# Step lists for fill, steady and drain turns, finer steps, and no filler matmuls, in a ViT tower on one core

## The chip, the cores and the metric

The kernel runs on one core of one Trainium2 chip. The metric is device time in microseconds (us), lower is better; three runs of the kernel before gave 623.52, 623.66 and 624.88 us.

## What is computed

128 images of 3x64x64 pass two transformer layers at 17 tokens (16 patches and a class token) of width 192. Cut to what matters:

```python
h = patches @ W_tok.T + b                         # 16 patches of 768 values, then cls in front
h = h + attn0(layernorm(h))                       # 12 heads of 64
    # dots = q k^T * scale; se = mean over heads; diagonal masked; top 12 of 17 kept; + se; softmax; @ v; @ w_out
h = h + bitlinear_ffn(layernorm(h))               # rmsnorm, int8 activations, ternary weights, 192 -> 2x512 -> 192
    # y = silu(gate) * up
h = h + attn1(layernorm(h))                       # gated linear attention, 12 heads of 16
    # params = silu(x Wb1) Wb2; gate = sigmoid(tanh(amp1 amp2 cos(phase difference)) temp)
    # num = q_f . cumsum(k_f v (1 + gate)); den = q_f . cumsum(k_f); layernorm per head of num / den; @ Wproj
h = h + ffn1(layernorm(h))                        # 192 -> 128 -> 192 -> 192, with a layernorm at the end
```

## The kernel before, in words

The tokens of 7 images are a group: 119 rows on the partitions. There are 19 groups, the last one of 2 images. A group passes six stages, and six groups are under way at once: in turn i the engines work on group i in stage 0, on group i-1 in stage 1 and so on to group i-5 in stage 5. `behind` is that distance. Stage 0: image strips, patches, embedding, first norm, q and v. Stage 1: k, scores, the top-12 search (`v_top`, `v_drop`, `v_mix`). Stage 2: softmax, attention, projection (`h1`). Stage 3: the quantised FFN (`h2`) and the norm, q, k, v and hidden gate layer of layer 1. Stage 4: the gate's parameters, linear attention, its projection (`h3`). Stage 5: the last FFN and the store.

Each engine has a list of its own, in program order: `iterations(engine, run, setup)` issues it and `in_turn` walks through its steps as (behind, step). One list serves all turns; in turns that lack a group the steps for it are left out. Turns 0 to 7 are written out (the filling ones), turns 8 to 17 are a loop over pairs, turns 18 to 23 are written out again (the draining ones). What crosses engines waits on a semaphore, one per step, counted by group. Within one engine, `chain_of` makes the next instruction of a chain wait for the one before it.

The part that matters below, of stage 4, for one group:

- PE `t_params` (L1546) gives the gate's parameters. ACT takes a tanh, POOL runs the chain `p_gate` (L581 to L597, 16 operations, wave to overlap), ACT `a_interference` makes tanh_over and tanh_int, and DVE `v_v1` (L903) scales v with it.
- PE `t_num` (L1580) multiplies by v, ACT copies, PE `t_num_turn` turns (L1181).
- DVE `v_ratio` makes num_sum, den and centred (L911 to L914), POOL squares centred (L603), DVE `v_sq_sum` (L919) sums, POOL `p_rstd_h` adds (L528) and takes the power -1/2 of 12 columns (L529, rstd_h), DVE `v_att1` (L923) multiplies, and PE `t_att1` turns the result for `t_proj1` (L1605).

In the steady list of the kernel before, DVE's `v_att1` stands behind `v_h1`, `v_u_in`, `v_h2` and `v_stats2`, and PE's `t_att1` stands behind `t_down`, `t_dots(0)`, `t_embed` and `t_dots(1)`.

The weights' setup (rounding to ternary values, gains, biases) stands on DVE in blocks between turns: `setup_ffn` (L680 to L684) behind turn 0's steps up to there, `setup_gains` (L691 to L698), and the biases with `late_setup`, a wait in which ACT and POOL too stand until the last setup word is out.

`zero_products` (L1186) issues on PE matmuls of zeros by zeros, 128x512 in bf16, into a PSUM bank that nobody reads at the time: 155 in all, in turns of groups 0 to 3 and 15 to 18, at the places named in PE's list.

The two lines on which the largest step below rests:

```python
dve.wait_ge(S["rstd_h"], g + 1)      # v_att1, line 922
pe.wait_ge(S["att1"], g + 1)         # t_att1
```

Of the kernel before, what the change touches and what calls it, by code (L numbers as in the profile page):

```python
# [35 lines left out]
EMBED = 192  # L36
PER = 7
# [73 lines left out]
def build(nc, a, table, out):  # L111
    ctx = ExitStack()
    with ctx:
# [3 lines left out]
        def sem(name):  # L117
# [189 lines left out]
        pad_drop = sb("pad_drop", [128, 1])  # L307
        pad = sb("pad", [128, 1])
        zeros = sb("zeros", [128, 512], BF16)
# [30 lines left out]
            a_done01 a_done2 a_masked0 a_masked1 a_masked2 num_done num_copied num den den_sq centred centred_sq sq_sum rstd_h  # L340
# [6 lines left out]
        RUN = {n: sem("run_" + n) for n in "v_att v_in v_out v_lin v_last p_ffn p_lin p_gate p_head p_last a_quant".split()}  # L347
# [56 lines left out]

        def for_group(pieces):

            def step(g, p):
                if isinstance(g, int) and g in pieces:  # L410
                    pieces[g]()
# [1260 lines left out]
```

## Time and profile before

| | |
|---|---|
| median of three runs | 623.66 us |
| the profiled execution, own time | 625.02 us |
| its span | 623.2 us |
| filling turns 0 to 7 | 0 to 214.5 us |
| ten steady turns, 8 to 17 | 214.5 to 496.5 us, 28.2 us each |
| draining turns 18 to 23 | 496.5 to 623.2 us |
| PE busy | 574.0 us (92%) |
| DVE busy | 463.4 us (74%) |
| ACT, POOL busy | 316.7 us (51%), 310.1 us (50%) |

The profile is of one execution, 1.36 us above the median. A turn is told from the next by the same instruction of the next group, for example PE's parameters matmul (L1546), which stands first in PE's list.

### The profile page before, as it was taken

The page shows a single profiled execution, that of the slowest core. Times are in us where ns is not written, and L with a number is a line of the kernel's source. Part 1 is how long each engine was busy: PE and PEld are TensorE (multiplying, and loading weights), DVE is VectorE, ACT ScalarE, POOL GpSimd, SP SyncE. Part 2 cuts the span into 40 slices and gives each one's busy share as a digit, 9 for nine tenths or more (in the row PEclk, how much of TensorE's full clock was granted, in tenths as well). Part 3 has the DMA queues.
Part 4 walks back from the last instruction along what each step waited for, and adds up shares of the span by engine and source line. Part 5 has one row for each costly group of instructions (what it writes and reads, how often), then busy time and mean ns, then how long its engine had stood idle before and what let it go on. Part 6 is the DMA issues. An engine that isn't in the chain of part 4 may idle for free.

```text
span 623.2 us, 15681 instructions
## 1 busy us (share of the span) xinstructions
PE 574.0 (92%) x5206; PEld 456.6 (73%) x5220; DVE 463.4 (74%) x2022; ACT 316.7 (51%) x849; POOL 310.1 (50%) x788
## 2 busy tenths in 40 slices
PE   4989899999999999999999999999999999988884
PEld 3667586878778787878878787878878787756451
DVE  0693676778797978888797978888797978775632
ACT  2244446573837465573838365564738364443310
POOL 2001033564647474655647474655656474644743
PEclk9999899999999999999999999999999999969977
DMA  8810000000100000000100000000000000000000
GB/s 233 191 61 1 24 24 0 25 24 2 29 8 24 8 23 8 25 28 0 28 6 22 6 22 6 22 19 9 12 6 0 6 2 7 2 7 1 7 7 8
DMA packets 11061, 14.69 MB, mean 24 GB/s; under 512 B 2159, under 2 KB 8656, under 8 KB 11016
## 3 DMA queue, kind: packets, MB, share of 16 engines
q1 hardware_dynamic: 8712, 12.44, 7.5%
q10 hardware_dynamic: 2304, 1.67, 1.0%
q8 instruction: 25, 0.41, 0.3%
q14 instruction: 20, 0.16, 0.1%
HBM read 12.44 MB, written 1.67 MB: 23 GB/s over the span
## 4 chain that ended last, share of the span: by engine, by line
DVE 32%; PE 30%; ACT 18%; issue 9%; POOL 8%; DMA 1%; DVEq 0%; SPq 0%; POOLq 0%; ACTq 0%
DVE kept L778 5%; ACT wide L1077 4%; PE bank_att L1321 4%; ACT probsT L1019 3%; PE bank_embed L1372 3%; DVE stats L729 3%; DVE top L770 3%; PE bank_lin L1526 2%; ACT patches L1027 2%; POOL rstd L529 2%; DVE scores L758 2%; ACT v L1053 2%; PE bank_att L1330 2%; ACT tanh_gate L1101 2%; PE bank_lin L1186 2%
## 5 line engine op out<-in xcount | busy, mean ns | idle before, releaser
L528 POOL TENSOR_TENSOR spread<-moments,gain_eps 119x1 f32<-119x1 f32 x57 | 11.6, 203 | 133.6 <-DVE moments L731 133.6
L529 POOL TENSOR_TENSOR rstd<-spread,minus_half 119x1 f32<-119x1 f32 (+1 forms) x95 | 55.5, 585 | 7.4
L1363 PE MATMUL bank_embed<-norm0T,w_qkv 128*128 128x119 f32 (+1 forms) x456 | 57.2, 275 | 1.7 <-ACT norm0T L1045 1.0
L1363 PEld LDWEIGHTS bank_embed<-norm0T,w_qkv 128*128 128x128 f32 x456 | 54.1, 192 | 2.5 <-ACT norm0T L1045 1.5
L1019 ACT COPY att1T<-bank_lin 96x238 f32<-96x238 f32 (+1 forms) x19 | 6.6, 347 | 79.3 <-PE bank_lin L1181 79.3
L558 POOL TENSOR_TENSOR scaled<-product,g_out 119x512 f32<-119x512 f32 x19 | 25.7, 1354 | 40.3 <-DVE product L853 40.3
L1306 PE MATMUL bank_embed<-w_tok,patchT 128*119 128x192 f32 (+1 forms) x228 | 43.9, 345 | 0.9 <-ACT patchT L1037 0.9
L529 POOL TENSOR_TENSOR rstd_h<-spread_h,minus_half 119x12 f32<-119x12 f32 x19 | 43.5, 2287 | 1.5
L1467 PE MATMUL bank_att<-w_o,att0T 128*119 128x192 f32 (+1 forms) x228 | 41.5, 332 | 0.0
L1306 PEld LDWEIGHTS bank_embed<-w_tok,patchT 128*119 128x119 f32 (+1 forms) x228 | 37.4, 186 | 3.7 <-ACT patchT L1037 1.1
L803 DVE TENSOR_TENSOR weightsT<-bank_lin,consts 119x476 f32<-119x476 f32 (+1 forms) x57 | 34.2, 627 | 6.7 <-PE bank_lin L1564 6.6
L1539 PE MATMUL bank_lin<-norms2T,w_qkv 97*128 97x119 f32 (+3 forms) x304 | 37.3, 276 | 0.0
L1467 PEld LDWEIGHTS bank_att<-w_o,att0T 128*119 128x119 f32 (+1 forms) x228 | 35.6, 179 | 1.2 <-ACT att0T L1019 0.3
L1539 PEld LDWEIGHTS bank_lin<-norms2T,w_qkv 97*128 97x128 f32 (+1 forms) x304 | 35.5, 191 | 0.6 <-ACT norms2T L1019 0.6
L758 DVE TENSOR_REDUCE scores<-bank_att 119x51 f32<-119x357 f32 (+1 forms) x76 | 34.9, 501 | 0.7 <-PE bank_att L1419 0.6
L1372 PE MATMUL bank_embed<-norm0T,w_qkv_rest 64*128 64x119 f32 (+1 forms) x456 | 35.2, 287 | 0.0
L1077 ACT ACTIVATE wide<-probs,consts 119x68 f32<-119x68 f32 x133 | 34.4, 352 | 1.3 <-DVE probs L794 1.3
L1564 PE MATMUL bank_lin<-feat_qk,feat_k 32*119 32x119 f32 (+1 forms) x456 | 34.1, 282 | 0.4 <-ACT tanh_par L1138 0.4
L778 DVE MATCH_REPLACE8 kept<-top,scores 119x20 f32<-119x20 f32 x228 | 34.1, 164 | 0.0
L1181 PE MATMUL bank_att<-consts,wide 119*119 119x119 f32 (+1 forms) x228 | 31.6, 276 | 2.2 <-DVE wide L814 1.8
L572 POOL TENSOR_TENSOR feat_k<-feat_qk,consts 128x238 f32<-128x238 f32 (+1 forms) x38 | 23.1, 627 | 21.0 <-DVE feat_qk L897 21.0
L1064 ACT COPY qkT<-bank_embed 128x357 f32<-128x357 f32 (+1 forms) x76 | 30.3, 457 | 6.3 <-PE bank_embed L1372 6.3
(247 smaller groups left out, 1525.8 us busy)
## 6 DMA issues: line engine op xcount, KB each, us to landing
strips<-x SPq DMA_DIRECT2D x18, 336.0 KB
out<-result ACTq DMA_DIRECT2D x18, 89.2 KB
w_qkv<-L_attn_w_qkv SPq DMA_DIRECT2D x2, 576.0 KB, 7.2
w_in_raw<-L_ffn_w_in SPq DMA_DIRECT2D x1, 768.0 KB, 11.6
w_tok_raw<-L_tok_W SPq DMA_DIRECT2D x1, 576.0 KB
w_qkv_rest<-L_attn_w_qkv SPq DMA_DIRECT2D x2, 288.0 KB, 8.9
w_o<-L_attn_w_out SPq DMA_DIRECT2D x1, 576.0 KB
w_qkv_raw<-L_attn_Wqkv SPq DMA_DIRECT2D x1, 432.0 KB
```

Source lines behind the costliest of these rows:

```text
L529: pool.tensor_tensor(rstd_out, spread, minus_half[0:ROWS, 0:spread.shape[1]], ALU.pow) \
L758: dve.tensor_reduce(scores[0:r, place:place + 3, TOKENS - 1::-1], parts(src, 3)[0:r, :, 0:r].rearrange("p h (b j) -> p h j b", j=TOKENS), ...
L778: last = dve.match_replace(kept[:, h, :], top[:, h, :], scores[:, h, :], BIG)
L803: dve.tensor_tensor(dst[0:r, :, 0:r], src[0:r, :, 0:r], mask[0:r, 0:r].unsqueeze(1).to_broadcast([r, 4, r]), ALU.mult).then_inc(ready_sem, 1)
L1077: last = act.activation(wide[:, 8:12, b], probs[:, 8:12, :], ACT.Copy, scale=block_mask[:, b * TOKENS:b * TOKENS + 1])
L1181: return pe.transpose(dst, src, identity)
L1306: last = pe.matmul(E0[0:r, 0:EMBED], patchT[:, k, 0:r], w_tok[:, k, :], start=k == 0, stop=k == CHUNKS - 1)
L1363: pe.matmul(parts((E0, E1)[s], 3)[:, j, 0:r], w_qkv0[:, tile * 128:(tile + 1) * 128], norm0T[:, s, 0:r], start=j == 0, stop=False, skip_gr ...
L1372: last = pe.matmul(parts((E0, E1)[s], 3)[:, j, 0:r], w_qkv0_rest[rows, n, j * 128:(j + 1) * 128], norm0T[rows, 1 - s, 0:r], start=False, s ...
L1467: last = pe.matmul(A1[0:r, 0:EMBED], att0T[:, t, 0:r], w_o0[:, t, :], start=t == 0, stop=t == QTILES - 1)
L1539: last = pe.matmul(parts(L1, 4)[:, j, 0:r], w_qkv1[0:rows, k, first:first + 128], norms2T[0:rows, 2 + k, 0:r], start=k == 0, stop=k == 1)
L1564: last = pe.matmul(lin[0:r, lin_column[slot]:lin_column[slot] + r], feat_k[32 * q:32 * q + 32, odd, t, 0:r], feat_qk[32 * q:32 * q + 32, t ...
```

## The change

- `iterations`, `in_turn` and `for_group` go. `program(eng, fill, steady, drain)` takes three lists for each engine: fill and drain of (group, step), steady of (behind, step). So the order of a filling or draining turn is no longer that of the steady one.
- Steps are cut finer (`v_top` in two, `v_ratio` into num_sum, den and centred, `p_gate` into wave, terms, series and overlap, `a_qk`, `t_proj0` and others in halves), each with a semaphore of its own where it needs one; other semaphores are merged (packed0 and packed1, for one). Steps of different groups stand between the parts of what was one chain.
- The setup is in pieces (`once(...)`), put between steps of the fill lists. The rounding of w_out (`setup_round_out`) and the gains and gates stand behind group 0's `v_wide1`, where before they stood ahead of group 0's scores and of its exp_sum; the waits of the late setup stand in group 2's part of each engine's list.
- No call of `zero_products` is left: all 155 matmuls of zeros go.
- The list of SP is as before. The arithmetic is that of before.

The diff, cut to its core, first of the common part:

```diff
-        def iterations(eng, run, setup):
...
+        def program(eng, fill, steady, drain):
 
             first = DEPTH + 1 + (DEPTH + 1) % 2
             end = first + (GROUPS - first) // 2 * 2
-            for i in range(first):
-                run(i, i % 2, [0 <= i - n < GROUPS for n in range(DEPTH)])
-                if i < len(setup):
-                    setup[i]()
+            for g, step in fill:
+                step(g, g % 2)
             with eng.Fori(0, (end - first) // 2) as pair:
...
+                for half in range(2):
+                    for behind, step in steady:
+                        step(2 * pair + (first + half - behind), (half + behind) % 2)
+            for g, step in drain:
+                step(g, g % 2)
```

POOL, the one list before, and the beginning of the steady list now:

```diff
-                (4, p_gate), (5, p_h3_beta), (3, p_scaled), (3, p_rms), (5, p_rstd4), (4, p_centred_sq), (1, p_h0),
-                (4, p_rstd_h), (3, p_rstd2), (2, p_rstd1), (0, p_rstd0), (4, p_rstd3), (3, p_feat_k),
...
+                (4, p_wave), (5, p_h3_beta), (4, p_terms), (1, p_h0), (4, p_series), (4, p_overlap), (3, p_scaled), (3, p_rms),
+                (4, p_centred_sq), (4, p_den_sq), (4, p_rstd_h), (2, p_rstd1), (3, p_rstd2), (5, p_rstd4), (0, p_rstd0), (4, p_rstd3),
```

DVE, a stretch of the list before, two lines of the filling list and two of the steady list now:

```diff
-                (4, v_causal[2]), (3, v_gated), (4, v_v1), (3, v_big_out), (4, v_ratio), (4, v_sq_sum), (2, v_h1), (2, v_u_in),
-                (3, v_h2), (3, v_stats2), (4, v_att1), (1, v_pack(1, A1)), (1, v_pack(0, A0)), (5, v_result), (3, v_norms2),
...
+                (0, once(setup_round_out)), (1, once(setup_gains(0))), (1, once(setup_gains(1))), (1, once(setup_gates)), (0, v_h1),
...
+                (3, v_att1), (5, v_stats1), (2, v_scaled4), (6, v_pack0), (4, v_h2), (4, v_stats2), (6, v_pack1), (4, v_moments2),
...
+                (4, v_centred), (4, v_sq_sum), (2, v_h1), (4, v_att1), (2, v_stats1), (2, v_moments1), (2, v_u_in), (3, v_h2),
+                (3, v_stats2), (3, v_moments2), (1, v_pack1), (1, v_pack0), (3, v_norms2), (5, v_moments4), (1, v_top0), (0, v_h0),
```

PE, two lines of the list before and two of the steady list now:

```diff
-                (3, zero_products(E0, {17: 2, 18: 2})), (3, t_down), (1, t_dots(0)), (1, zero_products(E0, {18: 9})), (0, t_embed),
-                (0, zero_products(L1, {2: 3})), (1, t_dots(1)), (4, zero_products(E0, {15: 2, 16: 10, 17: 10, 18: 10})), (4, t_att1),
...
+                (4, t_num_turn), (2, t_proj0_0), (2, t_proj0_1), (3, t_int_out), (0, t_patches1), (0, t_patches0), (4, t_att1),
+                (3, t_down), (1, t_dots0), (0, t_embed), (3, t_norms2), (1, t_dots1), (4, t_proj1), (3, t_qk1), (0, t_norm0), (3, t_hid),
```

Three places in the steady list show how rows move.

**PE, from the turn of int_out to proj1, before.** Names are out<-in; L1181 is the helper that turns (att: the att1 turn; norms: norms2), L1506 is down, L1413 and L1419 are the scores (dots), L1306 the embedding, L1605 proj1.

```order
L1181 MATMUL bank_ffn<-ident_b,int_out 128x119 x4
...
L1181 MATMUL bank_embed<-consts,patches 128x84 x8
L1506 MATMUL bank_ffn<-w_out,int_outT 119x192 x4
L1413 MATMUL bank_att<-mask_factors 119x357 x2
L1419 MATMUL bank_att<-qkT 119x119 x6
L1306 MATMUL bank_embed<-w_tok,patchT 119x192 x6
L1413 MATMUL bank_att<-mask_factors 119x357 x2
L1419 MATMUL bank_att<-qkT 119x119 x6
L1181 MATMUL bank_lin<-consts,att 96x119 x2
L1181 MATMUL bank_lin<-consts,norms 96x119 x4
L1605 MATMUL bank_lin<-w_p,att1T 119x192 x2
```

The same stretch of PE now (L1554 turns, L1868 is down, L1664 the embedding, L1964 proj1):

```order
L1554 MATMUL bank_ffn<-ident_b,int_out 128x119 x4
...
L1554 MATMUL bank_embed<-consts,patches 128x84 x8
L1554 MATMUL bank_lin<-consts,att 96x119 x2
L1868 MATMUL bank_ffn<-w_out,int_outT 119x192 x4
L1769 MATMUL bank_att<-mask_factors 119x357 x2
L1775 MATMUL bank_att<-qkT 119x119 x6
...
L1664 MATMUL bank_embed<-w_tok,patchT 119x192 x6
...
L1554 MATMUL bank_lin<-consts,norms 96x119 x4
L1769 MATMUL bank_att<-mask_factors 119x357 x2
L1775 MATMUL bank_att<-qkT 119x119 x6
L1964 MATMUL bank_lin<-w_p,att1T 119x192 x2
```

The att1 turn has moved ahead of down, the first scores, the embedding and the second scores.

**DVE, from the sum of squares to the first scores, before.** L825 is h1, L833 u_in, L869 h2, L923 att1.

```order
L919 TENSOR_REDUCE sq_sum<-centred_sq 119x12
L825 TENSOR_TENSOR h<-bank_att,h 119x192
L729 BN_STATS stats<-h 119x6
...
L833 SCALAR_TENSOR_TENSOR u_in<-h,moments,g_in 119x192
...
L835 TENSOR_REDUCE umax_in<-u_in 119x1
...
L869 SCALAR_TENSOR_TENSOR h<-bank_ffn,unit_out,h 119x192
L729 BN_STATS stats<-h 119x6
...
L731 BN_AGGR moments<-stats 119x2
L923 TENSOR_TENSOR att<-centred,rstd_h 119x192
```

The same stretch of DVE now:

```order
L1088 TENSOR_REDUCE sq_sum<-centred_sq 119x12
L938 TENSOR_TENSOR h<-bank_att,h 119x192
L1092 TENSOR_TENSOR att<-centred,rstd_h 119x192
L943 BN_STATS stats<-h 119x6
...
L953 SCALAR_TENSOR_TENSOR u_in<-h,moments,g_in 119x192
L1018 SCALAR_TENSOR_TENSOR h<-bank_ffn,unit_out,h 119x192
L1024 BN_STATS stats<-h 119x6
...
L801 BN_AGGR moments<-stats 119x2
```

The multiplication that waits for rstd_h has moved ahead of nine operations of groups in stages 2 and 3.

**POOL, the gate's chain, now.** h_beta is group i-5's, h (L534) is group i-1's; before, both stood outside the chain.

```order
L582 TENSOR_TENSOR wave_sq<-wave 119x12
L634 TENSOR_TENSOR h_beta<-h,beta 119x192
...
L586 TENSOR_TENSOR terms<-sine_odd,wave_sq 119x36
...
L589 TENSOR_TENSOR poly<-terms,sine_even 119x36
L590 TENSOR_TENSOR amps<-amp 119x12
L534 TENSOR_TENSOR h<-h,b_o 119x192
...
L594 TENSOR_TENSOR terms<-poly,wave 119x24
```

Two operations of 119x192 stand between links of the chain.

## Rows read from the trace of the kernel before

**Rows 1.** Windows: span, busy us (x instructions) of PE, PEld, DVE, ACT, POOL; PEclk, DMA, GB/s.

```profile
0.00:98.90 98.90, 82.76 (x617) 62.20 (x622) 54.43 (x246) 37.26 (x88) 14.03 (x53) 0.98 0.33 84
98.90:214.50 115.60, 110.83 (x1063) 92.57 (x1064) 94.80 (x420) 65.72 (x176) 63.91 (x157) 1.00 0.05 16
214.50:496.50 282.00, 271.99 (x2628) 228.55 (x2627) 234.76 (x1040) 163.66 (x440) 163.43 (x400) 1.00 0.05 14
496.50:623.20 126.70, 108.38 (x904) 73.32 (x910) 79.44 (x318) 50.02 (x146) 68.76 (x178) 0.90 0.02 5
```

**Rows 2.** Timeline of PE in one steady turn: start, us, line, out<-in, [idle before].

```profile
270.76 0.32 PE L1546 MATMUL bank_lin<-w_g,hidT 128*119 128x60 f32 x2
...
278.59 0.82 PE L1580 MATMUL bank_lin<-weightsT,v 119*32 119x119 f32 x24
...
284.19 0.54 PE L1506 MATMUL bank_ffn<-w_out,int_outT 128*119 128x192 bf16 x4
...
287.81 0.36 PE L1413 MATMUL bank_att<-mask_factors 64*119 64x357 bf16 x2
...
288.73 0.41 PE L1181 MATMUL bank_lin<-consts,att 119*96 119x119 f32 x2
288.97 0.57 PE L1181 MATMUL bank_lin<-consts,norms 119*96 119x119 f32 x4
...
290.75 0.42 PE L1181 MATMUL bank_embed<-consts,norm 119*128 119x119 f32 x2 [0.26 <-DVE norm L747]
...
294.73 0.88 PE L1526 MATMUL bank_lin<-w_qkv,norms2T 97*119 97x192 f32 x4 [0.43 <-DVE h L930]
...
299.02 0.32 PE L1546 MATMUL bank_lin<-w_g,hidT 128*119 128x60 f32 x2
```

**Rows 3.** Timeline of DVE in the same turn.

```profile
283.03 0.35 DVE L919 TENSOR_REDUCE sq_sum<-centred_sq 119x12 f32<-119x192 f32 x1 [0.62 <-POOL centred_sq L603]
283.44 0.36 DVE L825 TENSOR_TENSOR h<-bank_att,h 119x192 f32<-119x192 f32 x1
...
286.26 0.18 DVE L731 BATCH_NORM_AGGREGATE moments<-stats 119x2 f32<-119x6 f32 x1
...
286.35 0.33 DVE L923 TENSOR_TENSOR att<-centred,rstd_h 119x192 f32<-119x192 f32 x1
...
287.82 0.67 DVE L881 TENSOR_SCALAR norms<-h,moments,rstd 119x192 f32<-119x192 f32 x2
```

**Rows 4.** Timeline of POOL in the same turn.

```profile
276.76 0.59 POOL L618 TENSOR_TENSOR h_beta<-h,beta 119x192 f32<-119x192 f32 x1
...
283.50 0.21 POOL L528 TENSOR_TENSOR spread_h<-sq_sum,den_sq 119x12 f32<-119x12 f32 x1
283.79 2.29 POOL L529 TENSOR_TENSOR rstd_h<-spread_h,minus_half 119x12 f32<-119x12 f32 x1
286.51 0.22 POOL L563 TENSOR_TENSOR spread<-moments,gain_eps 119x2 f32<-119x2 f32 x1 [0.43 <-DVE moments L731]
```

**Rows 5.** Timelines of DVE and ACT: setup and what stood behind it.

```profile
31.44 0.75 DVE L680 TENSOR_SCALAR w_out_raw<-w_out_raw,w_scale_inv 96x1024 f32<-96x1024 f32 x1
...
33.81 0.53 DVE L758 TENSOR_REDUCE scores<-bank_att 119x51 f32<-119x357 f32 x1
...
42.16 0.51 DVE L691 TENSOR_SCALAR w_qkv<-w_qkv_raw,ln_wb 96x576 f32<-96x576 f32 x1
...
44.98 0.37 DVE L792 TENSOR_REDUCE exp_sum<-expd 119x12 f32<-119x204 f32 x1
...
66.73 0.37 DVE L786 TENSOR_TENSOR shifted<-mixed,least 119x204 f32<-119x204 f32 x1
...
70.29 0.37 ACT L1071 ACTIVATE expd<-shifted 119x204 f32<-119x204 f32 x1 [5.59 <-DVE pad L711]
```

**Rows 6.** Groups: the larger group of matmuls of zeros: busy us, mean ns | idle before.

```profile
L1186 PE MATMUL bank_embed<-zeros 128*128 128x512 bf16 x92 | 27.9, 438 | 0.7 <-issue 0.4
```

**Rows 7.** Window, columns as in rows 1, near the end of the drain.

```profile
598.90:605.70 6.80, 6.58 (x39) 2.93 (x38) 2.59 (x9) 0.80 (x4) 5.10 (x20) 0.50 0.03 10
```

More of the change, by code:

```diff
@@ L630, in _ @@
+            program(pool, fill, steady, drain)
         @block.vector
@@ new lines, in v_top, with step, v_fill @@
+            def v_top(n):
+                def step(g, p):
+                    dve.wait_ge(packed[n], 2 * g + 2)
+                    dve.memset(pads[0:ROWS, 5 + n:6 + n], 0.0)
+                    for h in heads_of(n):
+                        last = dve.max(top[:, h, :], scores[:, h, 0:TOKENS])
+                    last.then_inc(v_top_run[n], 1)
+                return step
+            def v_fill(n):
+                def step(g, p):
+                    dve.wait_ge(v_top_run[n], 2 * g + 1)
+                    dve.memset(top[:, :, DROP + 1:8].rearrange("p (x h) e -> p x h e", x=2)[:, :, 3 * n:3 * n + 3], FILLER) \
+                        .then_inc(v_top_run[n], 1)
+                return step
@@ new lines, in v_drop, with step @@
+            def v_drop(n):
+                def step(g, p):
+                    dve.wait_ge(v_top_run[n], 2 * g + 2)
+                    dve.memset(pad_drop[0:ROWS, n:n + 1], 0.0)
+                    for h in heads_of(n):
+                        last = dve.match_replace(kept[:, h, :], top[:, h, :], scores[:, h, :], BIG)
+                    last.then_inc(v_drop_run[n], 1)
+                return step
+            v_top_run = [RUN["v_top0"], RUN["v_top1"]]
+            v_drop_run = [RUN["v_drop0"], RUN["v_drop1"]]
@@ L976, in _ @@
+            program(dve, fill, steady, drain)
         @block.scalar
@@ L1071, in a_exp @@
                 act.activation(expd[:, :, :], shifted[:, :, :], ACT.Exp, scale=-1.0).then_inc(S["expd"], 1)
-            def a_wide(g, p):
-                act.wait_ge(S["probs"], g + 1)
-                after(act, S["turned2"], g)
-                for b in range(PER):
-                    last = act.activation(wide[:, 8:12, b], probs[:, 8:12, :], ACT.Copy,
-                                          scale=block_mask[:, b * TOKENS:b * TOKENS + 1])
-                last.then_inc(S["widened2"], 1)
@@ L1081, in _, with a_wide, step @@
-            a_probsT = [copy_step([(S["turned0"], S["turned1"], S["turned2"])[f]], probsT[:, 4 * f:4 * f + 4, :],
-                                  parts((A0, A1, A0)[f], 4)[0:ROWS], (S["probsT0"], S["probsT1"], S["probsT2"])[f]) for f in range(3)]
-            a_att = [copy_step([(S["att_done0"], S["att_done1"])[n]], att0T[:, 3 * n:3 * n + 3, :], parts((A1, A0)[n], 3),
-                               (S["att_copied0"], S["att_copied1"])[n]) for n in range(2)]
+            def a_wide(n):
+                def step(g, p):
+                    act.wait_ge(S["probs"], g + 1)
+                    after(act, S["turned2"], g)
+                    for b in ((0, 1, 2, 3), (4, 5, 6))[n]:
+                        last = act.activation(wide[:, 8:12, b], probs[:, 8:12, :], ACT.Copy,
+                                              scale=block_mask[:, b * TOKENS:b * TOKENS + 1])
+                    if n == 1:
+                        last.then_inc(S["widened2"], 1)
+                return step
@@ L1173, in _ @@
+            program(act, fill, steady, drain)
             act.wait_ge(stored[0], 16 * ((GROUPS + 1) // 2))
@@ L1658 @@
+            program(pe, fill, steady, drain)
 def kernel(**inputs):
```

762 lines of the change are left out of this document (541 added, 221 removed).

## The prediction

> **What bounds the kernel now.** I read the windows by stage first. The ten steady turns take 282.0 of 623.2 us, 28.2 each, with PE busy for 272.0 (96%), DVE for 235 and POOL for 163 at a granted clock of 1.00; the four filling turns from 98.9 to 214.5 take 28.9 each, and only the first 98.9 us and the last 126.7 us have PE idle for more than a seventh [rows 1]. So PE's own work sets the steady turn, and there is little to win there: its two waits of note are 0.26 and 0.43 us [rows 2]. What can be won lies at both ends; what can be lost is that one of PE's instructions moves ahead of the data it needs. For this I read the timeline of one steady turn on PE, DVE and POOL, with T = 270.76, where the parameters matmul starts, up to the next one at 299.02 [rows 2 to 4].
>
> **The steady turn: att1 comes too early.** Now PE's att1 turn stands right behind the patches, ahead of down. PE reached that place at 284.19, T+13.4 [rows 2]. But the data are not there: rstd_h, a power over 12 columns, takes 2.29 us on POOL and ends at 286.08, T+15.3 [rows 4]. It can't start earlier, since spread_h starts 0.12 us behind the end of sq_sum, and sq_sum waited for POOL's squares [rows 3, 4]. This whole chain hangs on the num turn, which keeps its place. Add DVE's multiplication, 0.33, and two hand-overs of about 0.1 (the gaps of 0.12 and 0.07 between sq_sum and spread_h and between moments and POOL's next spread, [rows 3, 4]): PE can start att1 at T+15.85 at the earliest. Before, it did so at 288.73, T+18.0, behind 4.5 us of other work, and did not wait [rows 2].
>
> On POOL two operations of 119x192 now stand between links of the gate's chain, which ends in the v that num (278.59) reads. h_beta took 0.59 [rows 4]; h has the same form. If both come in full, num is 1.2 us later, if they fill gaps between links, nothing. I take 0.5, since the strips copy that held ACT ahead of tanh_over has moved out of the way. So att1 starts at T+16.35 (ends 15.85 and 17.05).
>
> Behind it PE has what it had from 284.19 to 299.02, 14.83 us, less the two waits of 0.69 that the shift should swallow: 14.14 [rows 2]; the att1 turn itself (0.24, 288.73 to 288.97) is in it.
>
> DVE's list has the second half of the damage. Its multiplication stands right behind h1, so DVE stands from T+13.1 (h1 ends at 283.80) until T+15.9, and nine operations for h1's and h2's norms come after it. They took from 283.83 to 286.44, 2.6 us, of which umax_in (some 0.4, like sq_sum) has moved away; from the end of moments2 at 286.44 to the end of norms2 at 288.49 it was 2.05 more [rows 3]. Norms2 is then ready at T + 15.9 + 0.4 + 2.2 + 2.05 = 20.6. PE arrives there at 16.35 + 0.24 + 3.62 (284.19 to 287.81, [rows 2]) = T+20.2. So it waits 0.4 again.
>
> Turn: 16.35 + 14.14 + 0.4 = 30.9. I take off 0.3, because finer steps part links that stood next to each other: the two operations of norms2, with no wait between them, take 0.67 together [rows 3], 0.1 less than two of 0.38, whereas sq_sum and h1, with waits, start 0.41 apart for 0.35 of work. **30.6 us, 2.4 more than 28.2, ten times: +24 us.** Ends: 29.7 (nothing inserted counts, no wait for norms2), +15; 31.3, +31.
>
> The Trainium skill's page "VectorE: DVE Perf Modes", section "The DRAIN you can't avoid", has it that chained operations cost the same with and without a semaphore between them. By it the 0.3 falls away and the ten turns cost +27. The rows of norms2 speak for the smaller number.
>
> **Turns 4 to 7 of the fill.** Here too v_att1 stands ahead of some or all of h2, stats2 and moments2 on DVE, in turn 7 right behind h1. There PE's att1 stands later, behind down or the embedding, so most of the price comes by norms2: DVE stands up to 2.5 us. At 1 to 2.5 us a turn that is +7 for four. Against it: two turns' zeros go (some 2 us), and turns that took 28.9 have 0.7 us of slack each over the steady 28.2. Net **+4** (-4 to +10).
>
> **Turns 0 to 3.** Rounding of w_out took from 31.44 to 33.81, ahead of group 0's scores, and gains and gates 42.16 to 44.98, ahead of its exp_sum: 2.4 + 2.8 us of group 0's chain [rows 5]. Both now lie behind wide, where PE has probs, att0 and proj0 to do before DVE's h1. I count 4 of 5.2. The exponentials of group 1 started at 70.29, 3.2 us behind the end of shifted at 67.10, held by the setup's last word [rows 5]; now that wait stands a step later: -3. Zeros that stand in the way of ready work, and norm0 placed freely: -2. **-9** (-12 to -5).
>
> **The drain.** 92 of the matmuls of zeros have records with a mean of 438 ns, 27.9 us; they go into the embedding's bank, the ones of groups 15 to 18, so all of them stand here [rows 6]. Most lie in waits that stay. Taken out, those that overran their wait give back some 8. Turns 18 and 19 have v_att1 ahead of stats2 again (+4), and a turn of int_in now stands behind tanh_over on ACT (+1). **-3** (-12 to +10).
>
> SP's list is unchanged, and DMA is busy 2 to 5% of the time behind the first 98.9 us [rows 1]: nothing.
>
> **Sum:** -9 + 4 + 24 - 3 = +16. The profiled execution took 625.0, so 641.0 in its terms; the median of the runs is 1.4 below it, so **640 us**.
>
> **Rivals.**
>
> 1. *The cover holds, and it gets faster.* PE reaches att1 no earlier than its data, because it waits for something else before, which the trace before hides. Then v_att1 costs nothing in either list, the links and PE's small waits go (27.6 a turn, -6), and the ends give all they have (-12 in turns 0 to 3, nothing in 4 to 7, -7 in the drain): 625 - 25 - 1.4 = 599 us. It decides if PE arrives at T+15.9 or later without att1 having caused it. Against it: between num's turn and att1 PE has proj0, int_out's turn and the patches and nothing else, and it was dense there.
> 2. *Small stall, large gains at the ends.* The turn at its lower end, 29.7 (+15), with -11, -3 and -12 elsewhere: 625 - 11 - 1.4, 612 us.
> 3. *The clock falls without the zeros.* From 598.9 to 605.7 PE was 97% busy, much of it with zeros, and yet the granted clock was 0.50, the 1.2 GHz level; the whole drain had 0.90 [rows 1, 7]. If the drain is at 0.50 throughout from turn 19 on, some 35 us of real PE work there (of the drain's 108.4 - 27.9 = 80 us, [rows 1, 6], by the share of groups still under way, an estimate) take twice as long, and half of it lies on the path: +17, so 657 us. The steady turns would keep 1.00, as PE stays 89% busy. For it speaks the low clock even with zeros; against it, that work in the drain waits for DVE, ACT and POOL more than for PE. The Trainium skill's page "TensorE: Matmul & The Clock Gate", section "What's actually happening", says that the throttled state is the default and activity releases it. By that rule the removal is a loss at both ends of the kernel. By that rule alone PE, 97% busy there, should not have been at the lower level [rows 7]; so activity as such did not hold the clock here.
> 4. *Nothing lasting*: gains and losses cancel, within 0.2% of 623.66, by chance alone.
>
> **How the numbers follow.** My forecast (620 to 655) has 0.62, rival 1 0.12, rival 2 0.14, rival 3 0.09, rival 4 0.03. The range of 606 to 658 leaves out rival 1 and a part of rival 3. What a measurement can tell from no change is 0.2%, 1.25 us. Faster: rivals 1 and 2 and the low edge of the forecast, 0.27; same 0.04; slower 0.69.
>
> **What would show it.** In the profile after: PE's att1 turn in each steady turn with 2 to 3 us of idle before it, released by DVE's att, and DVE's att with as much, released by rstd_h; turns of 30.6 us, PE's busy share there near 89%; a smaller wait before the turn of norms2. The exponentials of groups 0 and 1 earlier by some 4 and 7 us. In the drain no zeros, and a clock near 0.9. If PE shows no idle before att1 in the steady turns, the forecast is wrong at its root; if the idle is there and the turn is still near 28, the rest of the turn was not dense.

## The result and the profile after

Four runs of the changed kernel took 652.87 to 660.17 us, median 658.57, against 623.59 (622.28 to 624.88, 4 runs) for the kernel before. The ratio is 1.0545, with a 95% interval of 1.0475 to 1.0614: 5.5% slower. The profiled execution took 659.78 us, its span 657.9. The forecast was 640 with a range up to 658. Where a median and a ratio below don't quite agree, it is because the ratios leave out runs that were disturbed.

Both traces are cut at the same marks: PE's parameters matmul of groups 0, 4 and 14, which open turns 4, 8 and 18. First the kernel before, windows (columns as in rows 1):

```profile
0.00:99.37 99.37, 83.23 (x619) 62.44 (x624) 54.43 (x246) 37.26 (x88) 14.03 (x53) 0.98 0.33 84
99.37:214.05 114.68, 109.91 (x1056) 91.89 (x1057) 94.39 (x419) 65.63 (x175) 63.91 (x157) 1.00 0.06 16
214.05:496.51 282.46, 272.45 (x2632) 228.99 (x2630) 235.19 (x1041) 163.75 (x440) 163.43 (x400) 1.00 0.05 14
496.51:623.20 126.69, 108.37 (x904) 73.32 (x910) 79.44 (x318) 50.02 (x146) 68.76 (x178) 0.90 0.02 5
```

The same four stages after, and then the last four parts of the drain (turns 19, 20, 21, and 22 with 23):

```profile
0.00:90.40 90.40, 72.16 (x564) 56.74 (x565) 53.11 (x264) 38.01 (x90) 12.88 (x51) 1.00 0.36 92
90.40:210.11 119.71, 109.87 (x1063) 93.61 (x1062) 91.40 (x430) 66.07 (x176) 63.61 (x159) 0.99 0.06 16
210.11:517.36 307.25, 276.06 (x2632) 240.14 (x2631) 230.50 (x1083) 165.95 (x440) 160.68 (x401) 0.96 0.04 13
517.36:657.90 140.54, 106.61 (x812) 79.80 (x810) 77.91 (x328) 48.17 (x144) 68.35 (x179) 0.68 0.02 5
...
548.93:576.78 27.85, 23.66 (x211) 20.46 (x209) 19.06 (x97) 12.25 (x36) 14.82 (x38) 0.78 0.01 2
576.78:606.15 29.37, 25.86 (x158) 18.75 (x158) 15.90 (x57) 11.41 (x35) 13.88 (x36) 0.56 0.03 7
606.15:630.29 24.14, 15.55 (x88) 9.37 (x88) 11.34 (x36) 5.88 (x17) 12.39 (x34) 0.50 0.02 4
630.29:657.90 27.61, 13.06 (x91) 8.99 (x91) 8.26 (x30) 2.65 (x11) 10.41 (x31) 0.50 0.03 8
```

The times of the stages, in us:

| stage | before | after | difference | forecast |
|---|---|---|---|---|
| turns 0 to 3 | 99.4 | 90.4 | -9.0 | -9 |
| turns 4 to 7 | 114.7 | 119.7 | +5.0 | +4 |
| ten steady turns | 282.5 | 307.3 | +24.8 | +24 |
| drain | 126.7 | 140.5 | +13.9 | -3 |

Three terms came out within 1 us, not all for the reasons that I gave. The fourth went the other way, and its row says where to look: the granted clock of the drain is 0.68 against 0.90, and 0.50, the 1.2 GHz level, in its last 52 us.

The steady turn on PE, timeline of the turn from 302.32 (L1908 parameters, L1939 num, L1868 down, L1775 scores, L1664 embedding):

```profile
302.32 0.32 PE L1908 MATMUL bank_lin<-w_g,hidT 128*119 128x60 f32 x2
...
311.14 0.82 PE L1939 MATMUL bank_lin<-weightsT,v 119*32 119x119 f32 x24 [1.26 <-DVE v L1061]
...
318.71 0.63 PE L1554 MATMUL bank_lin<-consts,att 119*96 119x119 f32 x2 [2.10 <-DVE att L1092]
319.14 0.85 PE L1868 MATMUL bank_ffn<-w_out,int_outT 128*119 128x192 bf16 x4
319.91 0.55 PE L1769 MATMUL bank_att<-mask_factors 64*119 64x357 bf16 x2
320.26 1.41 PE L1775 MATMUL bank_att<-qkT 64*119 64x119 f32 x12
321.60 2.41 PE L1664 MATMUL bank_embed<-w_tok,patchT 128*119 128x192 f32 x12
...
333.62 0.32 PE L1908 MATMUL bank_lin<-w_g,hidT 128*119 128x60 f32 x2
```

And on DVE in that turn:

```profile
315.92 0.36 DVE L938 TENSOR_TENSOR h<-bank_att,h 119x192 f32<-119x192 f32 x1 [0.30 <-PE bank_att L1823]
318.30 0.36 DVE L1092 TENSOR_TENSOR att<-centred,rstd_h 119x192 f32<-119x192 f32 x1 [2.02 <-POOL rstd_h L522]
```

The reader is to see two waits that [rows 2, 3] do not have: 2.02 us on DVE for rstd_h and 2.10 us on PE for att, the same wait seen twice. A third one, 1.26 us before num, comes of the two operations in POOL's gate chain, as a run below shows; it stands in seven of the ten turns. And behind the waits the twelve score matmuls, which took 0.79 us in the kernel before and take 0.79 later in this same turn, take 1.41.

That last one is the clock. Windows of this turn, of the next, and of two short stretches of this one:

```profile
302.32:333.62 31.30, 27.95 (x264) 24.39 (x263) 23.45 (x109) 16.58 (x45) 15.99 (x41) 0.95 0.05 14
333.62:363.85 30.23, 26.64 (x264) 23.03 (x263) 23.23 (x109) 16.59 (x45) 15.87 (x41) 1.00 0.05 14
...
320.00:323.00 3.00, 3.00 (x21) 2.79 (x22) 2.24 (x8) 0.07 (x1) 1.40 (x4) 0.66 0.00 0
323.00:326.00 3.00, 3.00 (x29) 2.68 (x28) 2.57 (x17) 0.55 (x1) 0.83 (x3) 1.00 0.00 0
```

Behind the wait the granted clock stands at 0.50, the 1.2 GHz level: cut finer, from 318.7 to 322.0, 3.3 us, with PE busy throughout, and then it is back at 1.00. That costs PE 1.3 us of busy time (27.95 against 26.64 for the same 264 matmuls), and this turn 1.1 us against the next one, which has the same waits of 2.10 and 1.26 us and no dip. Seven of the ten steady turns stand at 0.94 or 0.95 and take 30.3 to 31.4 us, the three at 1.00 take 30.23; the shorter ones of the seven (30.3 to 30.6) are those in which num did not wait and att1 came at T+15.3 to 15.5 in place of T+16.4 (T is again the start of the turn). The Trainium skill's page "TensorE: Matmul & The Clock Gate", section "What's actually happening", has activity release the throttle; here the dip follows a wait of 2 us in an engine that is otherwise busy, and not every such wait.

### The profile page after: what moved, and what is told of

The parts are those of the page before. It is cut to its first block and busy times, and to the rows that moved or that the text cites. A ratio compares the mean times of both kernels' runs of the same rounds, so it can differ in the third digit from the quotient of the medians.

```text
span 657.9 us, 15543 instructions
## 1 busy us (share of the span) xinstructions
PE 564.7 (86%) x5065; PEld 470.3 (71%) x5065; DVE 452.9 (69%) x2101; ACT 318.2 (48%) x849; POOL 305.5 (46%) x788
## 5 line engine op out<-in xcount | busy, mean ns | idle before, releaser
L1664 PE MATMUL bank_embed<-w_tok,patchT 128*119 128x192 f32 (+1 forms) x228 | 48.0, 367 | 0.9 <-ACT patchT L1320 0.9
L1664 PEld LDWEIGHTS bank_embed<-w_tok,patchT 128*119 128x119 f32 (+1 forms) x228 | 42.0, 206 | 3.8 <-issue 1.5
L1901 PE MATMUL bank_lin<-norms2T,w_qkv 97*128 97x119 f32 (+3 forms) x304 | 42.8, 300 | 1.4 <-ACT norms2T L1302 1.3
L1302 ACT COPY norms2T<-bank_lin 96x476 f32<-96x476 f32 (+1 forms) x19 | 10.2, 537 | 69.3 <-PE bank_lin L1554 69.3
L1901 PEld LDWEIGHTS bank_lin<-norms2T,w_qkv 97*128 97x128 f32 (+1 forms) x304 | 40.8, 213 | 3.8 <-ACT norms2T L1302 3.5
L1346 ACT COPY qkT<-bank_embed 128x357 f32<-128x357 f32 (+1 forms) x76 | 32.0, 445 | 20.4 <-PE bank_embed L1729 20.4
L551 POOL TENSOR_TENSOR scaled<-product,g_out 119x512 f32<-119x512 f32 x19 | 24.8, 1304 | 34.7 <-DVE product L990 34.7
L1554 PE MATMUL bank_lin<-consts,att 119*96 119x119 f32 (+1 forms) x38 | 9.2, 333 | 36.1 <-DVE att L1092 36.1
L1925 PE MATMUL bank_lin<-feat_qk,feat_k 32*119 32x119 f32 (+1 forms) x456 | 35.7, 292 | 1.6 <-DVE weightsT L916 1.3
L1925 PEld LDWEIGHTS bank_lin<-feat_qk,feat_k 32*119 32x119 f32 (+1 forms) x456 | 28.4, 190 | 9.3 <-DVE weightsT L916 3.3
```

Of the source, the lines that this page charges most:

```text
L551: pool.tensor_tensor(scaled[:, :], product[:, :], g_out[:, :], ALU.mult).then_inc(S["scaled"], 1)
L1346: act.copy(qkT[:, p, QTILES * n + 3 * s:QTILES * n + 3 * s + 3, 0:r], parts((E0, E1)[s], 3)[:, :, 0:r]) \
L1664: last = pe.matmul(E0[0:r, 0:EMBED], patchT[:, k, 0:r], w_tok[:, k, :], start=k == 0, stop=k == CHUNKS - 1)
L1901: last = pe.matmul(parts(L1, 4)[:, j, 0:r], w_qkv1[0:rows, k, first:first + 128], norms2T[0:rows, 2 + k, 0:r], start=k == 0, stop=k == 1)
L1925: last = pe.matmul(lin[0:r, lin_column[slot]:lin_column[slot] + r], feat_k[32 * q:32 * q + 32, odd, t, 0:r], feat_qk[32 * q:32 * q + 32, t ...
```

## Experiments

All are compared with runs of the kernel before on the same chip (medians 623.9 to 626.5 us). Stage times are cut at the marks above, from one trace of each kernel.

### Att1 late in the steady lists

The edit moves one step on three engines:

```diff
-                (4, v_centred), (4, v_sq_sum), (2, v_h1), (4, v_att1), (2, v_stats1), (2, v_moments1), (2, v_u_in), (3, v_h2),
-                (3, v_stats2), (3, v_moments2), (1, v_pack1), (1, v_pack0), (3, v_norms2), (5, v_moments4), (1, v_top0), (0, v_h0),
+                (4, v_centred), (4, v_sq_sum), (2, v_h1), (2, v_stats1), (2, v_moments1), (2, v_u_in), (3, v_h2),
+                (3, v_stats2), (3, v_moments2), (4, v_att1), (1, v_pack1), (1, v_pack0), (3, v_norms2), (5, v_moments4), (1, v_top0), (0, v_h0),
...
-                (3, a_int_out), (1, a_k_0), (3, a_out_T), (0, a_patchT0), (4, a_att1_T), (0, a_patchT1), (3, a_norms_T), (0, a_norm0T),
+                (3, a_int_out), (1, a_k_0), (3, a_out_T), (0, a_patchT0), (0, a_patchT1), (4, a_att1_T), (3, a_norms_T), (0, a_norm0T),
...
-                (4, t_num_turn), (2, t_proj0_0), (2, t_proj0_1), (3, t_int_out), (0, t_patches1), (0, t_patches0), (4, t_att1),
-                (3, t_down), (1, t_dots0), (0, t_embed), (3, t_norms2), (1, t_dots1), (4, t_proj1), (3, t_qk1), (0, t_norm0), (3, t_hid),
+                (4, t_num_turn), (2, t_proj0_0), (2, t_proj0_1), (3, t_int_out), (0, t_patches1), (0, t_patches0),
+                (3, t_down), (1, t_dots0), (0, t_embed), (4, t_att1), (3, t_norms2), (1, t_dots1), (4, t_proj1), (3, t_qk1), (0, t_norm0), (3, t_hid),
```

> The changed kernel with one step moved in the steady lists alone: DVE's att1 behind moments2, PE's att1 turn behind the embedding, ACT's copy of it behind both copies of patches. Theory (the early place of att1 costs 24.8 us in ten steady turns, 307.25 against 282.46): the steady turns come back to 28 us or a little under, so 658.6 - 26 = about 632 us, with PE's idle time before the att1 turn gone in these turns and the clock there at 1.00. Rival (the finer order as a whole is slower, or POOL's inserted operations are): the turns stay over 30 us and the total over 652. In between, 29 to 30 us a turn, if both play a part. The drain should stay at some 140 us in either case.

Measured: 638.25 us (ratio to before 1.0196, 1.0132 to 1.026). The ten steady turns take 287.7 us, the first of them 27.90 and the other nine 28.87, where the changed kernel has 307.3:

```profile
214.52:502.25 287.73, 266.52 (x2631) 230.59 (x2630) 231.62 (x1081) 165.59 (x440) 159.57 (x400) 1.00 0.04 13
```

The clock is back at 1.00 and no wait for att1 is left in the steady turns. So the place of att1 is worth 1.95 us a turn, some 20 of the 24.8 us. Turns at full clock differ by 1.4 us (30.23 against 28.87); the rest goes with the dips. Its place is not all: 28.87 is still above the 28.2 of before. Turn 7, whose list is untouched, took 35.9 us at a granted clock of 0.86, where the trace of the changed kernel has 32.0 at 1.00. So one stage can differ by 4 us between two traces of the same list. PE's waits in these ten turns say what is next (us in total, times, longest):

```profile
PE bank_lin L1939 <- DVE v L1061: 11.3, 9, 1.3
PE bank_lin L1554 <- DVE norms L1033: 9.2, 10, 1.1
```

### The gate's chain cleared, with att1 early and late

Both runs put the two inserted operations of POOL behind the chain:

```diff
-                (4, p_wave), (5, p_h3_beta), (4, p_terms), (1, p_h0), (4, p_series), (4, p_overlap), (3, p_scaled), (3, p_rms),
-                (4, p_centred_sq), (4, p_den_sq), (4, p_rstd_h), (2, p_rstd1), (3, p_rstd2), (5, p_rstd4), (0, p_rstd0), (4, p_rstd3),
+                (4, p_wave), (4, p_terms), (4, p_series), (4, p_overlap), (5, p_h3_beta), (3, p_scaled), (3, p_rms),
+                (4, p_centred_sq), (4, p_den_sq), (1, p_h0), (4, p_rstd_h), (2, p_rstd1), (3, p_rstd2), (5, p_rstd4), (0, p_rstd0), (4, p_rstd3),
```

> The changed kernel with POOL's steady list alone put back: h3_beta behind overlap, h0 behind den_sq, so that nothing stands between the links of the gate's chain. Theory (the inserted operations make num late, and num's lateness moves the whole chain to att1): the num matmul no longer waits for v in the steady turns, att1 comes 0.5 to 1.2 us earlier, turns from 30.7 to 29.6 to 30.2, total 658.6 - 5 to -11, about 650. Rival (what is won before num is lost again in a longer wait before att1): turns stay within 0.2 us of 30.7.

> The late att1 of the run steady_att1_late and the clear gate's chain together, steady lists only. With att1 late the turn was 28.87 with waits of 1.25 us before num and 0.91 us before the turn of norms2. Theory: num's wait goes, turns of 27.4 to 28.1, below the 28.2 of the kernel before, total about 626 to 630. Rival (norms2's wait grows by what num's gives back): turns of 28.5 to 28.9, total 635 to 639.

Alone: 653.01 us (1.044, 1.0372 to 1.0509), steady turns of 30.3. With att1 late: 628.4 us (1.0041, 0.9999 to 1.0084; ten runs, 624.9 to 637.4, the trace is of the lowest), turns of 27.87. The windows of the ten turns of either run:

```profile
210.79:513.76 302.97, 278.89 (x2632) 244.66 (x2630) 222.31 (x1083) 167.18 (x440) 161.37 (x401) 0.95 0.04 13
```

```profile
209.24:487.97 278.73, 266.23 (x2631) 230.83 (x2630) 221.53 (x1083) 167.43 (x440) 160.94 (x401) 1.00 0.05 14
```

The two operations cost 1.0 us a turn where att1 is late (28.87 to 27.87) and 0.4 on average where it is early: there PE still waits 2.4 us for att1, and the clock stands at 0.94 in nine of the ten turns. The tenth, at 1.00, took 29.23 us, 1.0 less than the turns at 1.00 of the changed kernel; so there too the two operations cost 1.0 us, and more dips took most of it back. With both repaired the new steady list is 0.4 us a turn faster than the list before (27.87 against 28.25). That is the finer steps and the other reorderings together; no run has the finer steps alone.

### Which engine's early place costs

PE late with DVE early, and PE early with DVE as late as it can be:

> The changed kernel with PE's att1 turn (and ACT's copy) late in the steady lists, but DVE's att1 still right behind h1. Theory (both engines pay, PE by its own wait and DVE by holding nine operations until 2 us later): PE's wait before att1 goes, but the turn of norms2 waits longer, some 2 to 2.5 us; turns of 29.6 to 30.4, total 648 to 656. Rival (only PE's place matters): turns of 28.9, total 638 as in steady_att1_late. If DVE's place is all, turns stay at 30.7.

> As pool_chain_clear (steady turns of 30.3 to 30.4 us, mostly with a dip of the clock), with DVE's att1 behind stats1, moments1 and u_in in place of right behind h1; PE's att1 turn stays early. Further down it can't go while PE's is early, since h2 waits for PE's down, which stands behind the att1 turn. So DVE works through most of the 2 us that it stood. Theory (with PE early, PE's own wait of 2.1 us is enough to cost all): PE's wait before att1 stays at 1.9 to 2.4 us and turns at 29.8 to 30.6, total 646 to 655. Rival (DVE's standing is the half that costs, as pe_late_dve_early hints, where it alone left turns of 30.8): turns of 28.4 to 29.4, total 632 to 642.

```diff
-                (4, v_centred), (4, v_sq_sum), (2, v_h1), (4, v_att1), (2, v_stats1), (2, v_moments1), (2, v_u_in), (3, v_h2),
+                (4, v_centred), (4, v_sq_sum), (2, v_h1), (2, v_stats1), (2, v_moments1), (2, v_u_in), (4, v_att1), (3, v_h2),
```

Either one alone is enough to keep the loss. The diff is of the second, which stands on top of pool_chain_clear; the first takes the lines of PE and ACT from steady_att1_late, and leaves DVE's. PE late and DVE early: 675.0 us (1.0789, 1.0705 to 1.0873), worse than the changed kernel. Its four runs went from 667.15 to 682.42; the two lowest alone, 667.15 and 671.49, would be 1.07. The trace is of the lowest: turns of 30.8 to 31.0, two of them 34.0 at a clock of 0.85; PE's wait for att is gone from the steady turns and has become one for the turn of norms2, 2.6 us at its longest, with the clock at 0.92:

```profile
210.21:524.92 314.71, 288.73 (x2632) 249.52 (x2630) 223.58 (x1085) 165.70 (x440) 162.24 (x402) 0.92 0.04 12
```

And its waits for norms2 over the whole run:

```profile
PE bank_lin L1554 <- DVE norms L1033: 26.8, 14, 2.6
```

My theory had the mechanism and too small a size (29.6 to 30.4). PE early and DVE in the middle: 653.61 us (1.0447, 1.0398 to 1.0496), steady turns of 30.15, against 30.3 in pool_chain_clear, so the work that DVE did while it would have stood bought next to nothing. DVE still stood for rstd_h in these turns, up to 1.2 us each, so its share is made smaller here and not taken out. Waits of the whole run:

```profile
PE bank_lin L1554 <- DVE att L1092: 38.5, 17, 4.9
DVE att L1092 <- POOL rstd_h L522: 27.6, 18, 2.7
```

### The early place in the kernel before

```diff
-                (4, v_causal[2]), (3, v_gated), (4, v_v1), (3, v_big_out), (4, v_ratio), (4, v_sq_sum), (2, v_h1), (2, v_u_in),
+                (4, v_causal[2]), (3, v_gated), (4, v_v1), (3, v_big_out), (4, v_ratio), (4, v_sq_sum), (2, v_h1), (4, v_att1), (2, v_u_in),
...
-                (3, v_h2), (3, v_stats2), (4, v_att1), (1, v_pack(1, A1)), (1, v_pack(0, A0)), (5, v_result), (3, v_norms2),
+                (3, v_h2), (3, v_stats2), (1, v_pack(1, A1)), (1, v_pack(0, A0)), (5, v_result), (3, v_norms2),
...
-                (3, zero_products(E0, {17: 2, 18: 2})), (3, t_down), (1, t_dots(0)), (1, zero_products(E0, {18: 9})), (0, t_embed),
-                (0, zero_products(L1, {2: 3})), (1, t_dots(1)), (4, zero_products(E0, {15: 2, 16: 10, 17: 10, 18: 10})), (4, t_att1),
+                (4, zero_products(E0, {15: 2, 16: 10, 17: 10, 18: 10})), (4, t_att1), (3, zero_products(E0, {17: 2, 18: 2})), (3, t_down), (1, t_dots(0)), (1, zero_products(E0, {18: 9})), (0, t_embed),
+                (0, zero_products(L1, {2: 3})), (1, t_dots(1)), 
```

> The kernel before with att1 moved to where the changed kernel has it: DVE right behind h1, PE right behind the patches, in every turn (one list serves all). Theory (the early place alone makes the stall): steady turns from 28.2 to 30.3 to 31 us with 2 us of idle time before PE's att1 turn, ten of them +21 to +28; fill and drain another +4 to +10; total 650 to 660. Rival (only the finer order or POOL's inserted operations make it): steady turns under 29, total under 632.

Measured: 686.66 us (1.0864, 1.0797 to 1.0931). The six runs spread from 677.38 to 753.12, and the trace is of one of 691.44. The steady turns have 31.1 us, +2.85 each, so the early place alone makes the stall, without finer steps and with all zeros in. Eight of the ten stand at a clock of 1.00 and take 30.7 us, 2.5 more than before, each with the wait of 2.4 us: so the stall costs most of this without any dip, and a wait of that length isn't always followed by one. Fill and drain lost more than I had allowed (turns 4 to 7 took 129.3 for 114.7), which is why the total passed 660.

```profile
230.51:541.51 311.00, 273.53 (x2631) 232.52 (x2630) 236.31 (x1041) 163.56 (x440) 162.80 (x400) 0.98 0.04 12
```

The wait for att over the whole run, of which each steady turn has 2.4:

```profile
PE bank_lin L1181 <- DVE att L923: 42.7, 19, 2.7
```

### The zeros: taken from the kernel before, given back to the changed one

> The kernel before without any matmul of zeros, order unchanged. Theory (clock): steady turns 28.2 as before, drain from 126.7 to about 138 at a clock near 0.7; turns 0 to 3 within 3 us of before; total about 635. Rival (the zeros held up ready work more than they held the clock): total 615 to 620, drain under 122. If the clock falls at the same places but nothing gets longer, the total stays at 624.

All calls of `zero_products` are out of PE's list of the kernel before, and nothing else. Measured: 640.87 us (1.0233, 1.0179 to 1.0287). The ten steady turns take 282.3 us as before, and the drain went from 126.7 to 139.1. The fill lost too: turns 0 to 3 are 2.2 us longer, and turns 4 to 7 1.5, all of it in turn 4, at a clock of 0.89 where it had 1.00:

```profile
217.71:500.01 282.30, 272.34 (x2631) 228.93 (x2630) 235.14 (x1041) 163.57 (x440) 162.85 (x400) 1.00 0.05 14
500.01:639.10 139.09, 104.89 (x812) 81.13 (x810) 79.74 (x318) 50.04 (x146) 68.53 (x178) 0.67 0.02 5
```

PE has 92 recorded matmuls fewer than in the drain of before and yet is busy for 104.9 us against 108.4: of the 27.9 us of zeros [rows 6], 24.4 came back as slower work at a clock of 0.67. The theory holds, and its rival, which was my own reckoning of the drain, falls.

> The changed kernel with the 100 matmuls of zeros of the drain put back, each ahead of the same step and group as in the kernel before; the rest as changed. Theory (the drain's 140.5 us against 126.7 come from the granted clock, 0.68 against 0.90, which falls without the zeros): clock of the drain back to about 0.9, drain 127 to 131 us, total about 647. Rival (the new order of the drain is what costs): drain 138 to 146 us, total 657 to 664, whatever the clock. The steady turns stay at 30.7 us.

```diff
+            def zero_products(count):
+
+                def step(g, p):
+                    pe.wait_ge(S["k_copied0"], GROUPS)
+                    multiply_zeros(E0, count)
+                return step
...
-                (15, t_att1), (15, t_proj1), (16, t_norms2), (16, t_qk1), (15, t_norm3), (16, t_hid), (15, t_hid1), (16, t_params),
+                (15, zero_products(2)), (15, t_att1), (15, t_proj1), (16, zero_products(4)), (16, t_norms2), (16, t_qk1), (15, t_norm3), (16, t_hid), (15, t_hid1), (16, t_params),
```

Measured: 660.44 us (1.0464, 1.0371 to 1.0557). The four runs took 650.10, 658.05, 662.83 and 728.81 us, and the trace is of the third, so the total says little here. In this trace the drain takes 135.8 us at 0.87, against 140.5 at 0.68:

```profile
525.13:660.90 135.77, 113.22 (x904) 74.61 (x910) 77.29 (x328) 48.20 (x144) 68.52 (x179) 0.87 0.02 5
```

That is 5 of 14 us, but it is not clear of noise. The drain's list is the same in the changed kernel and in the five runs above that move a step in its steady lists alone, and its six traces took 134.9 to 140.5 us at clocks of 0.73 to 0.68; the one with the zeros lies inside:

```profile
513.76:648.70 134.94, 99.50 (x812) 74.71 (x810) 77.38 (x328) 48.14 (x144) 68.05 (x179) 0.73 0.02 5
```

So in the hand-written order the zeros raise the clock, and between nothing and 5 us comes of it. The other 9 us against the kernel before stay with them in: the first turn alone has 31.4 us against 28.3, both at a clock of 1.00. There att1 stands ahead of stats2 on DVE, but PE's wait for att in that turn is 0.4 us, beside 0.7 for the copy of int_in and 0.6 for that of norms2, so att1 isn't shown to be what costs.

### Fill and drain in the repaired steady order

`from_turn` makes turns 4 to 7 and 18 to 23 from the repaired steady lists; the hand-written list stays for turns 0 to 3.

```diff
+        def from_turn(first_turn, end_turn, steady, done=()):
+            return [(i - behind, step) for i in range(first_turn, end_turn) for behind, step in steady
+                    if 0 <= i - behind < GROUPS and (i - behind, step) not in done]
```

> Late att1 and clear gate's chain in the steady lists, and turns 4 to 7 and the drain generated from the steady lists in place of the hand-written ones, with the 100 matmuls of zeros of the drain back ahead of the same steps. The hand-written list is kept for turns 0 to 3, where the changed kernel is 9 us ahead. Theory: 91 us for turns 0 to 3, 113 to 116 for 4 to 7, 275 to 281 for ten steady turns, 126 to 130 for the drain: total 607 to 618, faster than both kernels. Rival (the finer order is slower in fill and drain too, whatever att1 does): 622 to 632.

> As aligned_with_zeros (618.3 us, drain 130.0 at a clock of 0.92), but without any matmul of zeros. Theory (the clock of the drain hangs on the zeros in every order tried: 126.7 to 139.1 in the order before, 140.5 to 135.8 in the changed one): drain 136 to 142 us at a clock near 0.7, total 625 to 631. Rival (the aligned drain is dense enough to hold the clock by itself): drain 125 to 130, total 613 to 618.

With the 100 zeros of the drain: 618.33 us (0.9879, 0.984 to 0.9918), 1.2% faster than the kernel before. Without: 629.59 us (1.0083, 1.005 to 1.0116). Their drains:

```profile
487.15:617.10 129.95, 106.07 (x904) 73.13 (x910) 76.56 (x328) 48.58 (x144) 67.94 (x179) 0.92 0.02 5
```

```profile
486.10:627.50 141.40, 104.61 (x812) 81.21 (x810) 76.92 (x328) 48.76 (x144) 67.89 (x179) 0.67 0.02 5
```

Same order, same work: the zeros are worth 11.5 us of the drain in this order, 12.4 in the order before, and between nothing and 5 in the hand-written one. The generated turns 4 to 7 took 115.7 us against 119.7 for the hand-written ones.

### The next wait: norms2

```diff
-                (3, t_down), (1, t_dots0), (0, t_embed), (4, t_att1), (3, t_norms2), (1, t_dots1), (4, t_proj1), (3, t_qk1), (0, t_norm0), (3, t_hid),
+                (3, t_down), (1, t_dots0), (0, t_embed), (4, t_att1), (1, t_dots1), (3, t_norms2), (4, t_proj1), (3, t_qk1), (0, t_norm0), (3, t_hid),
...
-                (4, p_centred_sq), (4, p_den_sq), (1, p_h0), (4, p_rstd_h), (2, p_rstd1), (3, p_rstd2), (5, p_rstd4), (0, p_rstd0), (4, p_rstd3),
+                (4, p_centred_sq), (4, p_den_sq), (1, p_h0), (4, p_rstd_h), (3, p_rstd2), (2, p_rstd1), (5, p_rstd4), (0, p_rstd0), (4, p_rstd3),
```

> As aligned_with_zeros, with PE's turn of norms2 behind the second scores in place of ahead of them, and POOL's rstd2 ahead of rstd1. There PE waited 1.2 us a turn for norms2 and DVE 1.0 us for rstd2. Theory: the wait goes, turns of 27.85 become 26.9 to 27.3, ten steady turns 6 to 9 us less, total 607 to 612. Rival (another operand is late right behind, such as norm0 or the score search on DVE): turns within 0.3 us of 27.85, total 615 to 618.

> As norms_late, with the hand-written filling list kept up to turn 4, where it took 28.6 us against 32.3 in the aligned one, and the aligned lists from turn 5 on. Theory: 2 to 5 us less than norms_late. Rival (turn 4's gain is work put off to turn 5): within 1 us of norms_late.

Measured: 605.46 us (0.9673, 0.9636 to 0.971). The steady turn is 26.79 us, 1.06 less, and the ten of them are PE's work and nothing else, 267.2 of 267.9 us busy:

```profile
203.51:471.41 267.90, 267.15 (x2632) 230.31 (x2630) 221.22 (x1082) 168.97 (x441) 159.74 (x401) 1.00 0.05 14
```

With the hand-written list kept through turn 4: 604.42 us (0.9674, 0.9637 to 0.9712), no difference that counts. Turn 4 gained 1.1 us and turn 5 took 31.9 in place of 26.7, so the gain was put off, as the rival had it, and the fill as a whole lost 2.7. That the totals agree even so is the drain's doing, 128.4 us against 132.2, where turn 21 stood at a clock of 0.97 in one trace and 0.79 in the other.

## Why the prediction was wrong, point by point

- **"The steady turn: att1 comes too early"**: right in place and mechanism. The mean of 30.7 us for 30.6 is in part luck. In the turns at full clock, such as the one from 333.62, the turn was 30.23, 0.4 less than I had. Where it was longer, up to 31.4, the dip of the clock behind the wait made it so, which I didn't have: I took PE to keep 1.00 there, as 89% busy. Its other terms: att1 started at T+16.4 (318.71 - 302.32), as forecast, but by two misses that offset. Num was 1.0 us later than before (T+8.82 for 7.83), where I took 0.5 out of 0 to 1.2 for POOL's two operations, and from num to att1 it was 7.6 us, where my sum has 8.0. The second wait for norms2, which I put at 0.4 us, was 0.2 in the turns at 1.00 and none in the others, where slower matmuls gave norms2 the time; it came out at 0.9 to 1.2 us when att1 was late.
- **"Finer steps part links"**: I took 0.3 us a turn. With att1 late and the chain clear the new list has 27.87 against 28.25, which is of that size, but it holds other reorderings too, and no run parts them.
- **Turns 4 to 7**: +5.0 for +4, but the terms that I gave (7, less 2 and less 4 times 0.7) make +2, and the loss isn't where I put it. It is in turn 5 (31.3 us for 28.3), where PE waited 2.6 us for att and the clock stood at 0.95, and in turn 7 (32.0 for 28.1), where PE waited 1.9 for scores and 1.3 for norms2; the other two turns gained 1.8. The zeros, which I counted as a gain of 2, were worth 1.5 us there in the order before.
- **Turns 0 to 3**: -9.0 for -9, but not by the terms I gave. Group 0 gained almost nothing: its exponentials started at 45.74 instead of 43.29, later and not 4 us earlier, and its h1 at 55.17 instead of 55.98. Those of group 1 came 2.3 us earlier (68.03 for 70.29), not 7. I missed that the sums of the weights, now behind group 0's k and a patches turn on PE, made DVE stand 6.80 us and round w_in five microseconds later than before:

```profile
32.42 0.16 DVE L725 TENSOR_SCALAR w_scale<-bank_ffn 128x1 f32<-128x1 f32 x1 [6.80 <-PE bank_ffn L1581]
33.48 0.62 DVE L736 TENSOR_SCALAR w_in_raw<-w_in_raw,w_scale_inv 128x768 f32<-128x768 f32 x1
...
48.34 0.74 DVE L736 TENSOR_SCALAR w_out_raw<-w_out_raw,w_scale_inv 96x1024 f32<-96x1024 f32 x1
55.17 0.36 DVE L938 TENSOR_TENSOR h<-bank_att,h 119x192 f32<-119x192 f32 x1 [1.79 <-PE bank_att L1823]
```

  The gain came with group 1 (h1 at 78.35 instead of 84.13) and later. That zeros go, counted as part of a gain of 2 us, cost 2.2 us in the order before. I didn't take the other terms apart on the chip, so that the sum came out at -9 is luck as far as is known.
- **The drain, -3**: this is the step that failed; it was +13.9. I had counted the zeros as work that overruns waits and gives back 8 us when it goes, and took the clock to stay near 0.9 without them. In none of three orders did their removal give back more than 1 us. Taken out of the kernel before they cost 12.4 us, because the clock goes from 0.90 to 0.67; in the generated order 11.5; in the hand-written one nothing to 5, with the clock at 0.68 to 0.73 in place of 0.87. The other term, +5 for the new order, came to 9 with the zeros in, and to between -4 and +1 without them (139.1 us in the order before, 134.9 to 140.5 in the new one). So the two don't add, and the 13.9 can't be divided between them. Rival 3 had the mechanism: its +17 on top of my -3 makes +14 for the drain and 657 us, close to what came. I gave it 0.09. What I held against it, that the drain waits for other engines more than for PE, the windows had denied in part: PE was busy for 108 of 127 us [rows 1], 28 of them with zeros. The window at 0.50 with PE 97% busy [rows 7] I read as a sign that zeros don't hold the clock. They don't hold it always; with them the drain stood at 0.87 to 0.92, without them at 0.67 to 0.73.
- **What stays open**: of the 9 us that the hand-written drain costs with the zeros in, att1's place, the other reorderings and the clock are not told apart. The generated order, in which att1 is late, has 130.0 us, 5.8 less. What the 55 zeros of the fill would be worth in the changed order no run shows. Nor does any show why a wait of the same length is followed by a dip of the clock in one turn and not in the next.

## What to carry to other kernels

When a step moves ahead on one engine, trace its operand back through the other engines and compare that latency with the work that is left in front of the step; here some 3 us of work stood before a chain of 5 (from the end of the num turn at 313.9 to att1 at 318.7 in the turn shown), and ten turns paid for it. Put the consumer of a slow operation (2.29 us for 12 columns of a power) behind the work that is ready, on each engine that touches it: here one early place, on PE or on DVE, was enough to keep the loss. And filler matmuls in waits may be dear to remove: read the granted clock of the stretch with and without them before counting them as waste.

## What the hardware showed that I had not expected

- A wait of 2.1 to 2.3 us in an engine busy for some 89% of the time was followed, in seven of ten turns, by up to 3.3 us at the 1.2 GHz level; with waits of at most 1.3 us in the same turns (steady_att1_late) the clock stayed at 1.00. In the kernel before with att1 early it stayed at 1.00 in eight of ten turns, behind waits of 2.4 us.
- The zeros, 100 matmuls that all write to a bank nobody reads, were worth 11.5 to 12.4 us in a drain of 127 to 141 us in two orders; in a third they raised the clock as well, but brought 5 us at most.
- Without zeros the drain ran at 0.50 to 0.55 from its third turn to the end, in the order before and in the generated one alike, although PE was busy for 82% of the third turn (25.9 of 31.4 us) and 73% of the fourth.
